# Gated projection and fp8 feed-forward on one core: a second projection in three passes for more units, weight rounding spread differently over ScalarE, GpSimd and VectorE, and two batches kept in SBUF

## The reference, cut to what matters

```python
def cond(x, session_ids, channel_counts, seq_lens, W_sess, b_sess, W2, b2):      # x: 32 x 128 x 2048
    xm = x * cmask[:, :, None]                                  # channels past the batch's count are 0
    h = gelu(einsum('bct,bch->bht', xm, W_sess[session_ids]) + b_sess[session_ids][:, :, None])   # 256 hidden
    out = einsum('bht,hs->bst', h, W2) + b2[None, :, None]      # 128 outputs
    return out * tmask[:, None, :]                              # times past seq_len are 0

def ffn(o, weight, bias):                                       # weight: 2048 x 2048
    w_scale = 448 / max(|weight|);   w_q = e4m3(clip(weight * w_scale))
    o_scale = 57344 / max(|o|);      o_q = e5m2(clip(o * o_scale))
    return einsum('bsk,nk->bsn', o_q, w_q) / o_scale / w_scale + bias

out = x + ffn(cond(x, ...), weight, bias)
```

## Time and profile before

| | |
|---|---|
| median of 3 runs | 832.85 us (832.84 to 832.87) |
| profiled execution, its own time | 833.1 us |
| its span, first to last instruction | 831.3 us |
| PE busy | 825.8 us (99%) |
| PEld, the weight loads of PE | 479.9 us (58%) |
| DVE busy | 479.5 us (58%) |
| ACT busy | 345.9 us (42%) |
| POOL busy | 511.8 us (62%) |
| granted TensorE clock | 1.0 of full speed all the time |
| moved by DMA | 220.77 MB, 266 GB/s on average |

### The profile page before, as it was taken

How to read it: one execution, slowest core, us unless ns; L and a number is a source line. 1 busy time by engine, 2 the same in 40 slices (tenths; PEclk the granted TensorE clock), 3 DMA queues, 4 the chain that set the end, 5 groups by cost and what they waited for, 6 DMA issues and landing times.

```text
span 831.3 us, 10181 instructions
## 1 busy us (share of the span) xinstructions
PE 825.8 (99%) x3568; PEld 479.9 (58%) x3568; DVE 479.5 (58%) x499; ACT 345.9 (42%) x372; POOL 511.8 (62%) x238
## 2 busy tenths in 40 slices
PE   9999999999999999999999999999999999999998
PEld 5777777776767676765444444444444444444444
DVE  6989889788888888888553232323232323232322
ACT  7999999988888888973100000000000000000000
POOL 2899999899999999995983242424242423232322
PEclk9999999999999999999999999999999999999999
DMA  7988999877777877657974868686868686868682
GB/s 258 322 321 321 367 339 353 301 285 296 284 289 303 305 267 301 253 187 246 298 295 119 282 214 282 210 285 212 280 213 280 214 283 214 279 213 282 215 248 107
DMA packets 75008, 220.77 MB, mean 266 GB/s; under 512 B 37594, under 2 KB 40930, under 8 KB 55778
## 3 DMA queue, kind: packets, MB, share of 16 engines
q1 hardware_dynamic: 74080, 219.30, 74.5%
q10 hardware_dynamic: 898, 1.09, 0.4%
HBM read 143.04 MB, written 69.21 MB: 255 GB/s over the span
## 4 chain that ended last, share of the span: by engine, by line
PE 99%; issue 0%; POOL 0%; DVE 0%; ACT 0%; POOLq 0%
PE ps_h L1071 53%; PE ps_h L980 22%; PE ps_o L995 11%; PE ps_o L1011 8%; PE ps_o L1007 4%; PE ps_o L934 1%; PE ps_h L1047 0%; PE ps_o L1071 0%; PE ps_o L980 0%; PE ps_o L1065 0%; POOL time L518 0%; PE ps_o L940 0%; PE ps_h L1052 0%; DVE o_and_max L881 0%; ACT x_sb L702 0%
## 5 line engine op out<-in xcount | busy, mean ns | idle before, releaser
L1071 PE MATMUL ps_h<-wqT,x_sb 128*128 128x512 bf16 x1920 | 413.7, 378 | 0.2 <-ACT x_sb L702 0.2
L1071 PEld LDWEIGHTS ps_h<-wqT,x_sb 128*128 128x128 fp8e5 x1920 | 187.7, 98 | 224.4 <-ACT x_sb L702 0.3
L528 POOL TENSOR_TENSOR xl<-x_sb,xh 128x1024 fp32r<-128x1024 f32 x62 | 149.5, 2411 | 16.3 <-ACT xh L607 16.3
L980 PE MATMUL ps_h<-xh,whl 128*128 128x512 f32 x508 | 150.3, 417 | 0.4
L569 POOL TENSOR_TENSOR x_sb<-x_sb,bias_sb 128x2048 f32<-128x2048 f32 (+1 forms) x15 | 66.7, 4447 | 131.7 <-DMA x_sb<-in_x 131.7
L569 POOL TENSOR_TENSOR h<-h,bias_sb 128x2048 f32<-128x2048 f32 (+1 forms) x15 | 66.7, 4443 | 122.7 <-DMA h<-in_x 122.7
L881 DVE SCALAR_TENSOR_TENSOR o_and_max<-ps_h,scales,h 128x512 f32<-128x512 f32 (+1 forms) x59 | 44.0, 746 | 136.2 <-PE ps_h L1071 136.2
L881 DVE SCALAR_TENSOR_TENSOR o_and_max<-ps_h,scales,x_sb 128x512 f32<-128x512 f32 x59 | 44.2, 750 | 133.4 <-PE ps_h L1071 133.4
L980 PEld LDWEIGHTS ps_h<-xh,whl 128*128 128x128 f32 x508 | 94.2, 188 | 42.0 <-issue 21.7
L765 DVE SCALAR_TENSOR_TENSOR o_and_max<-ps_o,b_sb,steps 128x1024 f32<-128x1024 f32 (+1 forms) x65 | 82.2, 1264 | 29.0 <-PE ps_o L1011 27.1
L755 DVE TENSOR_TENSOR hl<-ps_h,hh 128x1024 fp32r<-128x1024 f32 x63 | 76.8, 1219 | 13.4 <-ACT ps_h L614 13.3
(11 more groups left out here) (101 smaller groups left out, 657.2 us busy)
## 6 DMA issues: line engine op xcount, KB each, us to landing
x_sb<-in_x SPq DMA_DIRECT2D x44, 1024.0 KB, 5.7
masked_out<-o_and_max SPq DMA_DIRECT2D x32, 1024.0 KB, 6.8
o_in<-masked_out SPq DMA_DIRECT2D x32, 1024.0 KB, 8.9
...
```

The lines of the kernel that those rows point to most:

```text
L528: pool.tensor_tensor(xl[:, u % 2, :], x_cols(u), xh[:, u % 2, :].bitcast(fp32), ALU.subtract)\
L980: mm = nc.tensor.matmul(to[:, cols], whl[:, b % SLOTS_W, rows], xs[:, u % 2, cols], start=(k == 0), stop=(k == 2))
L1071: mm = nc.tensor.matmul(bank, q[:, k // 2, :, k % 2], wq[:, n, k, cols], start=(k == 0), stop=(k == KT - 1))
```

## The change

1. `SPLIT_H1` becomes units 2 to 28. A new list `SPLIT_BEHIND` holds two of every three units from 29 to 61 (those with u % 3 other than 1; 22 units). For these, ACT applies gelu1 twice (into `hh1_behind`, and back into PSUM), **DVE** makes the remainder `hl1_behind` from PSUM, in one buffer only, and PE issues six three-pass matmuls. `hidden(u+1, 1)` then waits for that remainder too, since it stands in the same PSUM tile.
2. The rounding constant is made differently. ACT writes `wc = |weight| * w_up` in bf16 (`w_up` is `w_scale * 2**20`) in place of `ws`; POOL bounds it from both sides in place (`lift_constant`, one TENSOR_SCALAR, 128 x 768 bf16); DVE makes `ws = weight * w_scale + wc` in one SCALAR_TENSOR_TENSOR with both tensors in SBUF (`add_round_at`); POOL subtracts `wc` as before. DVE's two exponent instructions and POOL's add are gone.
3. DVE's `add_round_at` stands behind `split_h_rest`, and in a `SPLIT_BEHIND` unit `scan_o` stands behind that.
4. Masking late session weights moves from ACT to POOL (one TENSOR_SCALAR, 128 x 256, every second unit).
5. QUANT is 28, so 33 chunks are rounded early and 10 late. The order of POOL's work between the stages is new.
6. The last two batches (30 and 31) stay in `o_sb`. They are neither stored nor loaded again and come first in the second stage (`batch_at`), and their x is still in SBUF, so that it isn't loaded again either. Buffers move accordingly: `q8` lives where `h1` was.

The core of the diff:

```diff
-    SPLIT_H1 = [u for u in range(2, 27)]
+    SPLIT_H1 = [u for u in range(2, 29)]
+    SPLIT_BEHIND = [u for u in range(29, UNITS - 2) if u % 3 != 1]
...
-    QUANT = SCANS + 2
+    QUANT = SCANS + 4
...
-    QUAD = 4
+    QUAD, KEPT = 4, 2
...
+        def batch_at(p):
+            return B - KEPT + p if p < KEPT else p - KEPT
...
-                if u % UPB == 0 and b > 0:
+                if u % UPB == 0 and 0 < b <= B - KEPT:
                     sp.wait_ge(o_masked, u)
                     store_o(b - 1)
...
+            def lift_constant(i):
+                c = wc[:, i % 2, 0:chunk_cols(i)]
+                pool.wait_ge(w_raised, i + 1)
+                pool.tensor_scalar(c, c, 2.0 * E4M3_MAX * ROUND_AT, 1.5 * E4M3_MIN_NORMAL * ROUND_AT, ALU.min, ALU.max)\
+                    .then_inc(w_floored, 1)
             def round_chunk(i):
                 v, c = ws[:, i % 2, 0:chunk_cols(i)], wc[:, i % 2, 0:chunk_cols(i)]
-                pool.wait_ge(w_round_ready, i + 1)
-                pool.tensor_tensor(v, v, c, ALU.add).then_inc(w_added, 1)
                 pool.wait_ge(w_added, i + 1)
                 pool.tensor_tensor(wqT[:, CHUNK_AT[i]], v, c, ALU.subtract).then_inc(w_rounded, 1)
...
+            def mask_session_weight(b):
+                wh = whl[:, b % SLOTS_W, 0:HID]
+                pool.wait_ge(whl_loaded[b % 2], ((b - DIRECT) // 2 + 1) * 16)
+                pool.tensor_scalar(wh, wh.bitcast(fp32), cmask[:, b:b + 1], 1.0, ALU.mult, ALU.mult).then_inc(whl_masked, 1)
...
                 if 0 <= u - QUANT - 1 < EARLY_CHUNKS:
                     round_chunk(u - QUANT - 1)
+                if 0 <= u - QUANT < EARLY_CHUNKS + 1:
+                    lift_constant(u - QUANT)
+                if u % UPB == 1 and DIRECT <= (u + 3) // 2 < B:
+                    mask_session_weight((u + 3) // 2)
...
             pool.wait_ge(bias_loaded, 16)
-            pool.wait_ge(x2_loaded[0], 16)
             add_bias(x2[0], FRONT)
+            round_chunk(late[0])
+            lift_constant(late[1])
+            pool.wait_ge(xl_ready, UNITS)
+            add_bias(x2[1], FRONT)
+            lift_constant(late[2])
+            pool.wait_ge(q_ready, CUTS)
...
+                if u in SPLIT_BEHIND:
+                    act.activation(hh1_behind[:, u % 2, :], ps_h[:, 1, :], ACT.Gelu, bias=hbias[:, 1, b:b + 1])
+                    act.activation(ps_h[:, 1, :], ps_h[:, 1, :], ACT.Gelu, bias=hbias[:, 1, b:b + 1])\
+                       .then_inc(h1_gelu, 1)
+                    return
...
-                act.activation(ws[:, i % 2, 0:chunk_cols(i)], wt[:, at:at + chunk_cols(i)], ACT.Copy, scale=w_scale)\
-                   .then_inc(w_scaled, 1)
+                act.activation(wc[:, i % 2, 0:chunk_cols(i)], wt[:, at:at + chunk_cols(i)], ACT.Abs, scale=w_up)\
+                   .then_inc(w_raised, 1)
...
+            def split_h1_behind(u):
+                dve.wait_ge(h1_gelu, u + 1)
+                if u == SPLIT_BEHIND[0]:
+                    dve.wait_ge(wl_later, DIRECT - UPB)
+                dve.tensor_tensor(hl1_behind[:, :], ps_h[:, 1, :], hh1_behind[:, u % 2, :].bitcast(fp32), ALU.subtract)\
+                   .then_inc(hl1_behind_ready, 1)
...
+            def add_round_at(i):
+                c, at = wc[:, i % 2, 0:chunk_cols(i)], i % 3 * CHUNK
+                dve.wait_ge(w_floored, i + 1)
+                dve.scalar_tensor_tensor(ws[:, i % 2, 0:chunk_cols(i)], wt[:, at:at + chunk_cols(i)], w_scale, c,
+                                         ALU.mult, ALU.add).then_inc(w_added, 1)
...
+                    if u in SPLIT_BEHIND and u - 1 in SPLIT_BEHIND:
+                        dve.wait_ge(o_psum, u)
+                        split_h1_behind(u)
                     mask_o(u - 1, start, 0, slice(0, UNIT))
+                    if u in SPLIT_BEHIND and u - 1 not in SPLIT_BEHIND:
+                        split_h1_behind(u)
...
+                    if u not in SPLIT_BEHIND:
+                        scan_o(u - 1, 0, slice(0, UNIT))
                 if u + 1 < UNITS:
                     split_h_rest(u + 1)
+                if 0 <= u - QUANT - 1 < EARLY_CHUNKS + 1:
+                    add_round_at(u - QUANT - 1)
+                if u in SPLIT_BEHIND:
+                    scan_o(u - 1, 0, slice(0, UNIT))
...
                 elif u > 0:
                     pe.wait_ge(h1_gelu, u)
+                    if u - 1 in SPLIT_BEHIND:
+                        pe.wait_ge(hl1_behind_ready, SPLIT_BEHIND.index(u - 1) + 1)
...
+                elif u in SPLIT_BEHIND:
+                    for j, (w, hs) in enumerate(((w2l1, hh1_behind[:, u % 2, :]), (w2h1, hh1_behind[:, u % 2, :]),
+                                                 (w2h1, hl1_behind))):
```

More of the change, by code:

```diff
@@ L120, in adaln_ffn @@
         o_max = sb("o_max", [P, UNITS + 1], fp32)
-        scales = sb("scales", [P, 10], fp32)
+        scales = sb("scales", [P, 11], fp32)
         w_pmax, w_rec, w_scale, w_inv = (scales[:, k:k + 1] for k in range(4))
-        o_pmax, o_amax, o_rec, o_scale, o_inv, y_scale = (scales[:, k:k + 1] for k in range(4, 10))
+        o_pmax, o_amax, o_rec, o_scale, o_inv, y_scale, w_up = (scales[:, k:k + 1] for k in range(4, 11))
         wqT = sb("wqT", [P, WCOLS], bf16)
         x_sb = sb("x_sb", [P, 2, T], fp32)
+        raw_at = -(-nc.sbuf_base // 32) * 32
         raw = sb("raw", [P, SLOTS_W, HID], fp32)
+        assert SLOTS_W * HID == UNIT
         whl = sb("whl", [P, SLOTS_W, 2 * HID], fp32r)
@@ L443, in _ @@
             turn(1)
-            for r in range(2):
-                sp.wait_ge(o_stored[r], 2 * 16)
-                load_o(2 + r, r)
-            for r in range(2):
-                sp.dma_start(x2_more[r][:, FRONT], x[2 + r, :, FRONT]).then_inc(x2_more_loaded[r], 16)
+            load_x_more(1)
             for b in range(2):
@@ L572, in _ @@
             pool.wait_ge(bias_loaded, 16)
-            pool.wait_ge(x2_loaded[0], 16)
             add_bias(x2[0], FRONT)
-            for i in late[0:2]:
+            round_chunk(late[0])
[4 more added lines that the diff above has]
+            pool.wait_ge(q_ready, CUTS)
+            for b in range(KEPT):
+                pool.tensor_tensor(x3[:, b, :], x2[b][:, FRONT.stop:F], bias_sb[:, FRONT.stop:F], ALU.add).then_inc(x3_ready, 1)
+            for i in late[1:7]:
                 round_chunk(i)
-            pool.wait_ge(x2_loaded[1], 16)
-            add_bias(x2[1], FRONT)
-            for i in late[2:6]:
-                round_chunk(i)
+                lift_constant(i + 2)
             pool.wait_ge(x2_more_loaded[0], 16)
             add_bias(x2_more[0], FRONT)
-            for i in late[6:]:
+            for i in late[7:]:
                 round_chunk(i)
+                if i + 2 < CHUNKS:
+                    lift_constant(i + 2)
             pool.wait_ge(x2_more_loaded[1], 16)
@@ L587, in _ @@
             pool.wait_ge(x3_loaded, 16)
-            for b in range(QUAD):
+            for b in range(KEPT, QUAD):
                 pool.tensor_tensor(x3[:, b, :], x3[:, b, :], bias_sb[:, FRONT.stop:F], ALU.add).then_inc(x3_ready, 1)
@@ L632, in scale_chunk @@
                 at = i % 3 * CHUNK
-                act.activation(ws[:, i % 2, 0:chunk_cols(i)], wt[:, at:at + chunk_cols(i)], ACT.Copy, scale=w_scale)\
-                   .then_inc(w_scaled, 1)
-            def mask_session_weight(b):
-                wh = whl[:, b % SLOTS_W, 0:HID]
-                act.wait_ge(whl_loaded[b % 2], ((b - DIRECT) // 2 + 1) * 16)
-                act.activation(wh, wh.bitcast(fp32), ACT.Copy, scale=cmask[:, b:b + 1]).then_inc(whl_masked, 1)
+                act.activation(wc[:, i % 2, 0:chunk_cols(i)], wt[:, at:at + chunk_cols(i)], ACT.Abs, scale=w_up)\
+                   .then_inc(w_raised, 1)
             def high_session_weight(b):
@@ L704, in _ @@
                    .then_inc(q_widened, 1)
-            for i in range(EARLY_CHUNKS + 2, CHUNKS):
-                scale_chunk(i)
-                if UNITS - QUANT + 2 <= i + 3 < CHUNKS:
-                    act.wait_ge(w_scaled, i + 1)
+            for i in range(EARLY_CHUNKS + 1, CHUNKS - 1):
+                if i > EARLY_CHUNKS + 1:
+                    scale_chunk(i + 1)
+                if i + 3 < CHUNKS:
+                    act.wait_ge(w_added, i + 1)
                     at = i % 3 * CHUNK
@@ L902, in _ @@
                        .then_inc(y_ready, 1)
-                if y in CHUNK_BEHIND and 4 + CHUNK_BEHIND.index(y) < len(late):
+                if y in CHUNK_BEHIND:
                     i = late[4 + CHUNK_BEHIND.index(y)]
-                    exponents(i)
-                    round_at(i)
+                    add_round_at(i)
             def step2(i, last):
@@ L1007, in project1 @@
                             mm = nc.tensor.matmul(ps_o[:, u % 2, cols], w[:, :], hs[:, u % 2, cols],
+                                                  start=False, stop=(j == 2))
+                elif u in SPLIT_BEHIND:
```

(4 more changed lines are left out.)

125 lines of the change are left out of this document (51 added, 74 removed).

## The result

The changed kernel takes **844.91 us** (median of 4 runs, 844.02 to 846.47), the one before 832.86 us (4 runs). The ratio is 1.0148, 95% interval 1.0135 to 1.016: 12 us slower, where 2.6 us faster was forecast, and outside the range. The profiled execution took 844.52 us with a span of 842.7, so 11.4 us of span are to be found.

A forecast was written before the change was run, and what follows sets the result against it. PE bounds the kernel before, POOL with the port shared with DVE the changed first stage. The first stage's -5.0 us, the end's +1.8 and 0.6 given back make -2.6 us: 830.3 us, range 826.8 to 838.

The forecast's parts named there:

- the ring: First stage: POOL's remainder of x (`xl`), DVE's add, then POOL's subtraction, lift and half a mask in series, 5.74 us a unit.
- the term of 0.68 us for the lift: First stage, POOL: bounding 768 bf16 columns at 0.82 ns each, 0.63 us, plus 0.05 us between starts.
- a lift over 0.8 us: Sign in the changed profile that the forecast is wrong; TENSOR_SCALAR on 128 x 768 was expected near 0.7 us.
- rest of the add, and handover: First stage: 0.80 us of DVE's scale-and-add left after POOL's `xl` ends, plus 0.08 us until POOL's subtraction.
- second rival: First stage: a dearer lift takes POOL's chain past 5.90 us a unit and the kernel is slower; chance 0.27.
- The turning point: First stage: the lift time, 0.76 us, above which POOL's chain makes the kernel slower, 3.3 us per 0.1 us.
- 5.0 us gained: First stage: 5.3 us from 33 units and 0.4 from units 27 and 28, less 0.7 for queues out of step.
- 0.6 given back: First stage: allowance of 0.6 us for ACT starts that may slip, taken off the gain.
- The exclusion: First stage: DVE's scale-and-add, reading two SBUF tensors, and a POOL instruction block each other whole; add at 1.4 to 1.9 us.
- POOL is not the bound: Rival, first stage: no exclusion or a lift nearer 0.4 us; PE and ACT set 5.70 us, 827.8 us; chance 0.18.
- The end of the first stage: Stage boundary: chunk 33's scale-and-add waits for POOL's bias add and delays DVE's mask; 1.8 us lost, bounds 0 and 3.
- the lift is dearer, and the kernel slower: Rival, first stage: POOL's chain passes 5.90 us a unit, each 0.1 us of lift costing 3.3 us; chance 0.27.

The follow-up runs named there:

- half a lift: Changed kernel with POOL's lift on only the first 384 of each chunk's 768 columns: 834.87 us, ratio to the kernel before 1.002.
- the masks: Changed kernel with the masks of the session weights back on ACT in place of POOL: 838.1 us, ratio to the kernel before 1.0068.
- the run with one input: Changed kernel with DVE's scale-and-add replaced by a one-input AND of exponent bits, POOL subtracting from a constant tensor, weights not rounded: 828.56 us.
- the ring is loosened: Changed kernel without POOL's lift, the rounding constant left unbounded: 828.66 us, ratio to the kernel before 0.9949.

## Why the prediction was wrong

**The mechanism was the one forecast, the sizes were not.** The step that failed is the sum of the ring, 5.74 us a unit, and in it above all the term of 0.68 us for the lift. The prediction had named a lift over 0.8 us as a sign of being wrong, and it took 0.83:

| link, us a unit | forecast | measured |
|---|---|---|
| `xl` | 2.41 | 2.40 |
| rest of the add, and handover | 0.88 | 0.90 |
| subtraction, start to start | 1.61 | 1.75 |
| lift, start to start | 0.68 | 0.91 |
| mask, every second unit | 0.16 | 0.21 |
| sum | 5.74 | 6.17 |

More than half of the 0.43 is the lift. It was priced from what a bf16 tensor saves in a two-tensor instruction, 0.82 ns a column, and nothing was put down for the part that doesn't depend on the width. The same paragraph has that part: 0.18 us, in "2.18 x 768 + 0.18". The two widths run here give (827 - 506) / 384 = 0.84 ns a column and 0.19 us fixed, so the column was right, and 0.63 + 0.18 = 0.81 us would have been within 0.02 of the measured 0.83. That is 0.20 us of it. The mask has the same gap: 0.28 forecast, 0.46 with the 0.18, 0.48 measured. The iota's 0.84 us for 768 columns, which the prediction set aside for "may be short by 0.15", came within 0.02. That can be luck, since its split into a fixed part and columns isn't known.

The second error is one of the time between instructions. The 1.61 us of the subtraction are its 1.66 less the 0.05 by which `xl` overlapped it. Around the lift nothing overlaps: 0.08 us lie free ahead of it (240.94 to 241.02) and behind it (241.85 to 241.93). That makes 0.14 us at the subtraction and 0.03 at the lift. The prediction could have seen such distances, if not this one: in the kernel before, 0.08 us lie free between POOL's addition and its subtraction each time, both two-tensor instructions.

```profile
364.56 1.64 POOL L535 TENSOR_TENSOR ws<-ws,wc 128x768 f32<-128x768 f32 x1
366.28 1.66 POOL L537 TENSOR_TENSOR wqT<-ws,wc 128x768 bf16<-128x768 f32 x1
```

So it isn't the number of tensors that decides, and what does stays open: behind the mask, which has one tensor, `xl` overlaps by 0.04 us (247.90 + 0.48, 248.34). The prediction also took the 0.05 with two signs, added to the lift's 0.63 and the mask's 0.28, and taken off the iota's 0.84 in its second rival. With one sign, the iota's price makes that kernel 4.3 us slower, not 1.

The Trainium skill (GPSIMD Engine Reference, section "Elementwise — side-by-side cycle accounting") gives 1.03 cycles a column for a body of at most two operations. The rows agree for the column alone, 0.84 ns being 1.0 cycle at the 1.2 GHz assumed; the time of the whole instruction is 0.83 us against the 0.66 estimated from that page of the skill, since the fixed part comes on top, and the measurement decides.

**From the pace to the time.** The turning point was put at a lift of 0.76 us with all else as forecast, at 3.3 us for each 0.1 us. The experiments bear the slope out: half a lift, 0.32 us, is worth 10.6 us up to the first product (10.6 by the rule), the masks 6.8 us. What the first stage lost, 8.25 us, stands against 5.0 us gained, less 0.6 given back: 12.65 of the 14.0 us between the forecast span (828.7) and the measured one (842.7). The end (3.05 for 1.8) and 0.1 behind it are the rest.

**The exclusion** of the scale-and-add and POOL was argued from L872 and held (no waiting: 1.01 us; in the ring: 1.83 on average). The Trainium skill (SBUF — State Buffer, section "Who interferes with whom") says the same, and the run with one input agrees: 0.94 us, never over 0.96. So "POOL is not the bound" is refuted.

**ACT**: right that it is not the bound of this kernel. It and PE come next: 98.3 and 99.9 of 100 us once the ring is loosened, with a pace of 5.72. **DVE**: the add 1.02 us by sum, 1.01 measured.

**The end of the first stage** was forecast at 1.8 us with bounds of 0 and 3, and came to 3.05. The order on POOL and DVE was as described; POOL reached the bias add at the same time as DVE reached `hl`, not 1.06 us ahead of it (374.6 against 375.66), since POOL runs behind DVE in the slower ring. And the lower clock behind PE's idle time wasn't in the sum, 0.4 us here. What the prediction didn't see is that this wait has another one behind it: the run with the bias adds moved gave its 3 us back.

**Kept batches**: 0 forecast; the whole second stage, late chunks included, came 0.1 us longer.

**The rival that came true** is the one on the other side, "the lift is dearer, and the kernel slower", with a chance of 0.27. By its own rule a lift 0.23 us dearer gives 830.3 + 7.6 = 837.9 us, the upper end of the range; the other 0.20 us of the ring's 0.43 brought it out of the range. The range had been drawn with one link uncertain, and three were (lift, subtraction and mask).
